# Fixed regions per expert in the dispatched rows, and the meeting of all engines moved ahead of the last group's normalisation

## The reference, cut to what matters

```python
x = x + ga * attn(h)                      # retention and an MLP of 1024: x3 in the kernel
h = _layernorm(x) * (1 + cb) + sb         # h3
probs = softmax(h @ gate_w.T)             # 16 experts
topk_w, topk_idx = top_k(probs, 4)        # weights, then divided by their sum
shared = silu_mul(h @ shared_gate_up.T, 704) @ shared_down.T * sigmoid(h @ shared_gate_vec.T)
sparse = sum over experts e of silu_mul(h @ w_gu[e].T, 176) @ w_d[e].T * combine[:, e]
out = x + gb * (shared + sparse)
```

## Time and profile before

| what | us |
|---|---|
| median of three runs | 632.84 (631.92 to 635.31) |
| the profiled execution, its own time | 636.92 |
| its span (first to last instruction) | 635.1 |
| PE busy, DVE busy, ACT busy, POOL busy | 541.8, 473.5, 283.3, 321.8 |
| mean granted clock of PE | 0.928 of full |

### The profile page before, as it was taken

The page is one execution under the profiler, slowest core; times in us unless marked ns, Lnnn a source line. Parts: engine busy times, 40 slices in busy tenths (PEclk is TensorE's granted clock), DMA queues, the critical chain, the costliest instruction groups (busy, mean ns, idle before and its releaser), DMA issues.

```text
span 635.1 us, 14023 instructions
## 1 busy us (share of the span) xinstructions
PE 541.8 (85%) x4139; PEld 471.7 (74%) x4140; DVE 473.5 (75%) x1197; ACT 283.3 (45%) x696; POOL 321.8 (51%) x390
## 2 busy tenths in 40 slices
PE   4889899999979999994799789977999999999600
PEld 1567677888869889882587568866999999999500
DVE  3588989888743898987675876756777777777478
ACT  3355555556546655441245244425444444444200
POOL 3256776878665474551076757700444444444400
PEclk8889999999999999995789989978999999999855
DMA  9412122224990521112166567686544444442297
GB/s 309 162 57 71 55 73 83 52 74 149 329 311 14 148 76 62 49 58 68 42 186 201 166 212 232 221 252 209 167 133 130 125 132 127 124 131 88 76 382 279
DMA packets 66389, 92.30 MB, mean 145 GB/s; under 512 B 8512, under 2 KB 55360, under 8 KB 66336
## 3 DMA queue, kind: packets, MB, share of 16 engines
q1 hardware_dynamic: 56176, 69.72, 36.2%
q0 software_dynamic: 6864, 18.88, 8.0%
q10 hardware_dynamic: 3296, 3.03, 1.4%
HBM read 53.69 MB, written 35.82 MB: 141 GB/s over the span
## 4 chain that ended last, share of the span: by engine, by line
PE 34%; DVE 8%; issue 4%; DMA 3%; ACT 2%; another core or an unknown queue 1%; SPq 0%; POOL 0%; DVEq 0%; ACTq 0%; POOLq 0%
PE bank L2063 12%; PE bank L1797 5%; PE bank L2081 4%; DVE wda_lo L2028 4%; PE bank L1813 3%; PE bank L2083 3%; PE bank L2047 3%; PE bank L2073 3%; DMA wgu_hi<-results 1%; ACT s_a_hi L1604 1%; DMA stage<-expert_d 1%; DMA stage<-expert_gu 1%; DVE s_a_lo L1720 1%; DMA stage<-shared_d 0%
## 5 line engine op out<-in xcount | busy, mean ns | idle before, releaser
L1931 POOL DMA_INDIRECT results<-yb,xe x79 | 75.8, 959 | 107.1 <-DVE yb L2010 75.6
L1575 POOL DMA_INDIRECT dispatched<-rows,slot x64 | 66.0, 1031 | 40.1 <-issue 17.5
L2063 PE MATMUL bank<-wgu_hi,xT_hi 128*128 x158 | 59.2, 375 | 5.5 <-DVE xT_lo L1991 5.5
L2004 DVE TENSOR_TENSOR e_hT_lo<-bank,e_hT_hi 128x256 fp32r<-128x256 f32 x79 | 33.5, 425 | 32.6 <-issue 20.5
L2063 PE MATMUL bank<-wgu_hi,xT_lo 128*128 x158 | 51.9, 329 | 0.0
L2063 PE MATMUL bank<-wgu_lo,xT_hi 128*128 x158 | 51.9, 329 | 0.0
L736 DVE TENSOR_TENSOR probs<-bank,causal 128x512 f32<-128x512 f32 x64 | 39.8, 684 | 13.6 <-PE bank L926 13.6
L1964 ACT CAST e_hT_hi<-bank 128x256 fp32r<-128x256 f32 x79 | 29.4, 373 | 41.1 <-PE bank L2073 37.9
L1959 ACT ACTIVATE e_sg<-bank 128x176 f32<-128x176 f32 x79 | 25.1, 317 | 50.1 <-PE bank L2063 34.1
L591 POOL TENSOR_TENSOR orms<-omse,neghalf 128x16 f32<-128x16 f32 x16 | 47.1, 2944 | 0.3
L1797 PE MATMUL bank<-h3T_hi,wsg_hi 128*128 128x512 f32 x88 | 38.3, 435 | 6.3 <-DVE hid L1716 2.1
(11 more groups left out here) (234 smaller groups left out, 1854.9 us busy)
## 6 DMA issues: line engine op xcount, KB each, us to landing
dispatched<-fill SPq DMA_DIRECT2D x20, 520.0 KB, 9.0
xe<-dispatched SPq DMA_DIRECT2D x79, 130.0 KB
trig<-t_trig SPq DMA_DIRECT2D x16, 512.0 KB, 3.7
stage<-expert_gu SPq DMA_DIRECT2D x16, 352.0 KB
wgu_hi<-results SPq DMA_DIRECT2D x11, 512.0 KB, 7.7
xt<-L_attn_x SPq DMA_DIRECT2D x32, 128.0 KB, 2.6
wgu_lo<-results SPq DMA_DIRECT2D x5, 512.0 KB, 16.5
x_rows<-h_all SPq DMA_DIRECT2D x16, 128.0 KB, 2.0
```

The lines of the kernel that those rows point to most:

```text
L1575: pool.indirect_dma_start(out=dram["dispatched"], out_offset=bass.IndirectOffsetOnAxis(ap=slot[:, k, t:t + 1], axis=0), in_=rows[:, t, :], ...
L1931: pool.indirect_dma_start(out=dram["results"], out_offset=bass.IndirectOffsetOnAxis(ap=xe[r][:, E:E + 1].bitcast(INT), axis=0), in_=yb[:, ...
L2004: nc.vector.tensor_tensor(hT[1][:, q, :], hT_bank[p][:, 0:2 * P], hT[0][:, q, :].bitcast(F32), ALU.subtract).then_inc(S["h_lo"], 1)
L2063: mm = nc.tensor.matmul(gu_bank[p][:, 0:GU], xT[xn_][:, p, k, :], wgu[wn][:, k, e, :], start=(k == 0 and i == 0), stop=(k == KB - 1 and i ...
```

## The change

Each expert gets a region of its own of REGION = N + P = 2176 rows in `dispatched` (16 regions, and 16 tiles of empty rows behind them). A slot is then the region's start plus the row's rank among the rows of that expert so far, and is known for the first EARLY = 10 tiles as soon as those are ranked. The functions of the row chain move out of `mlp` into `normalised_rows`, which is built twice: for the first block, and again for the second (`last`). The meeting now stands ahead of the row chain of group 3, and that chain is laid between the first blocks of the shared expert. The ranking is in two parts (10 tiles, 6 tiles), as are `slots` and the scatters, which no longer wait for PE's products. The counts are turned into tile numbers by PE with four small products; the 16 steps of `experts_of_tiles` are gone, and each tile has a row number (`tile_row`) that SP reads into a register ahead of each load. Only 4 DMAs write filler at the start. For each expert SP writes 128 rows behind its last one (`fill_up`), at an address from a register, in two DMAs. The splits of the shared down weights go from DVE to POOL. The 24 pieces are 0, 6, 9 and 9 in the four groups.

```diff
+REGION = N + P
+EMPTY = NX * REGION
+EARLY = NT - TPG - 2
-        ("dispatched", (ETILES * P, ROW)), ("results", (N * TOPK + 4 * P, E)), ...
+        ("dispatched", (EMPTY + NX * P, ROW)), ("results", (N * TOPK + (4 + NX) * P, E)), ...
 # mlp, SP
-        for n in range(ETILES // 4):
+        for n in range(NX // 4):
             sp.dma_start(unused[n, :, :, :], fill[:, :, :]).then_inc(s_filled, 16)
-            store(NT - TPG + i, i)
 # mlp, POOL, ACT, DVE and PE: the row chain of group NG - 1 is gone from the end of each
-        for i in range(TPG):
-            inverse_std(NG - 1, i)
...
-        for i in range(TPG):
-            evacuate(NG - 1, i)
...
-        for i in range(TPG):
-            add_residual(NG - 1, i)
-        for i in range(TPG + 1):
-            finish(NG - 1, i)
...
-        for i in range(TPG):
-            transpose_h3(NG - 1, i)
-            route(NG - 1, i)
 # shared_and_dispatch
-        count = [[0, 0, 1, 1, 1, 1], [1] * 6, [1, 2, 1, 2, 1, 1], [1] * 6]
+        count = [[0] * 6, [1] * 6, [2, 1, 2, 1, 2, 1], [2, 1, 2, 1, 2, 1]]
 # SP
+        def fill_up(e):
+            if e == 0:
+                sp.wait_ge(S["free"], 1)
+            row = sp.value_load(first_free[0:1, e:e + 1], min_val=0, max_val=EMPTY)
+            sp.dma_start(dram["dispatched"][bass.ds(row, P), 0:E], gb[:, :]).then_inc(s_filled, 16)
+            with nc.allow_non_contiguous_dma(reason="one index per row"):
+                sp.dma_start(dram["dispatched"][bass.ds(row, P), E:E + 1].bitcast(INT), unfilled[:, e:e + 1]).then_inc(s_filled, 16)
+
         def body(g, q):
             for b in range(NB):
+                if g == 1 and b >= 2:
+                    for e in range((b - 2) * NX // 4, (b - 1) * NX // 4):
+                        fill_up(e)
                 if g and b == 4:
                     for n in range(TPG):
                         store_x4(g - 1, n)
                 for n in pieces(g, b):
                     load_piece(n)
 # POOL
+        last.inverse_std(LG, 0)
+        last.inverse_std(LG, 1)
         pool.wait_ge(S["tab_in"], 64)
+        number(0, near)
+        number(0, far)
+        low_down(0)
+        last.inverse_std(LG, 2)
+        last.inverse_std(LG, 3)
+        low_down(1)
+        send(0, near, 1, 1)
+        low_down(2)
+        send(0, far, 2, 1)
+        for k in range(1, TOPK):
+            number(k, near)
+            send(k, near, 2 * k + 1, k + 1)
...
-                    if n % PACE == 0:
-                        pool.wait_ge(S["g_ps"], n // PACE + 2)
 # DVE
+        def first_blocks():
+            for i in range(TPG):
+                last.add_residual(LG, i)
+            for i in range(2):
+                last.stats(LG, i)
+                last.centre(LG, i)
+            rank_early()
+            last.modulate(LG, 0)
+            last.keep_logits(LG - 1, TPG - 1)
+            last.compare(LG - 1, 1)
+            product(0, 0)
+            slots(0, False)
+            last.stats(LG, 2)
+            last.centre(LG, 2)
+            last.modulate(LG, 1)
+            low_hidden(0, 0)
+            last.choose(LG - 1, 1)
+            last.stats(LG, 3)
+            last.centre(LG, 3)
+            last.modulate(LG, 2)
+            last.modulate(LG, 3)
+            last.low_part(LG, 0)
+            last.keep_logits(LG, 0)
+            product(0, 1)
+            last.low_part(LG, 1)
+            last.keep_logits(LG, 1)
+            low_hidden(0, 1)
+            slots(1, False)
+            last.compare(LG, 0)
+            hidden(0, 2)
+            last.low_part(LG, 2)
+            last.keep_logits(LG, 2)
+            last.choose(LG, 0)
+            slots(2, False)
+            last.low_part(LG, 3)
+            last.keep_logits(LG, 3)
+            last.compare(LG, 1)
+            last.choose(LG, 1)
+
         def route(g, b):
-            if g == 0 and b == 0:
-                bases()
-                slots(0)
-                low_down(0)
...
+            if g == 0 and b == 3:
+                tiles_of_experts()
+                slots(3, False)
+                rank_late()
+                slots(0, True)
             elif g == 0 and b == 4:
+                ends_of_experts()
                 less_best()
+                slots(1, True)
+            elif g == 0:
+                slots(2, True)
             elif g == 1 and b == 0:
+                experts_of_tiles()
                 shared_gate()
+                slots(3, True)
             elif g == 1 and b < 5:
-                experts_of_tiles(b - 1)
                 weigh(b - 1)
 # PE: group 0
+        first_product(0, 0)
+        early_ranks()
+        pe.wait_ge(S["first"], 1)
+        last.transpose_h3(LG, 0)
+        first_product(0, 1)
+        last.transpose_h3(LG, 1)
+        last.route(LG, 0)
+        second_product(0, 0, 0)
+        first_product(0, 2)
+        last.transpose_h3(LG, 2)
+        last.route(LG, 1)
+        second_product(0, 1, 0)
+        last.transpose_h3(LG, 3)
+        last.route(LG, 2)
+        first_product(0, 3)
+        last.route(LG, 3)
+        second_product(0, 2, 0)
+        first_product(0, 4)
+        count()
+        first_product(0, 5)
+        second_product(0, 3, 0)
+        base_of_experts()
 # experts_and_combine, SP
-                sp.dma_start(xe[r][:, :], dispatched[j, :, :]).then_inc(s_in[r], 16)
+                row = sp.value_load(tile_row[0:1, bass.ds(j, 1)], min_val=0, max_val=EMPTY + (NX - 1) * P)
+                sp.dma_start(xe[r][:, 0:E + 1], dispatched[bass.ds(row, P), 0:E + 1]).then_inc(s_in[r], 16)
```

More of the change, by code:

```diff
@@ L1078, in mlp @@
     ahead = Ahead()
+    R = normalised_rows(nc, sem, wait, alone, neghalf, ident, modb, h_all, near, early, h3T, rows, logits, order, chosen, before_tile,
+                        ebefore, x3_tiles, outs, b_tr, b_lg, 0, S)
     def chunk(n):
@@ L1435, in shared_and_dispatch, with rows_from @@
-def shared_and_dispatch(nc, io, sb, sem, wait, alone, bank, gb, weights, tile_expert, h3T, rows, logits,
-                        order, chosen, before_tile, ebefore, wsg, wgu, dram, s_filled, s_down, home):
+        R.route(NG - 2, TPG - 1)
+    def rows_from(first):
+        return normalised_rows(nc, sem, wait, alone, neghalf, ident, modb, h_all, near, early, h3T, rows, logits, order, chosen, before_tile,
+                               ebefore, x3_tiles, outs, b_tr, b_lg, first, None)
+    return Stage(sync, gpsimd, scalar, vector, tensor, S, ahead, rows_from)
@@ L1438, in shared_and_dispatch @@
+def shared_and_dispatch(nc, io, sb, sem, wait, alone, bank, gb, weights, tile_expert, tile_row, h3T, rows, logits,
+                        order, chosen, before_tile, ebefore, wsg, wgu, dram, s_filled, s_down, home, last):
     INT = mybir.dt.int32
     NB, LAST = SBLOCKS, SBLOCKS - 1
+    bank = [bank[n] for n in (0, 3, 5, 7, 1, 4, 2, 6)]
+    LG = NG - 1
     RING, SKEW = 3, 2
@@ L1765, in body @@
                 hidden(g, b)
-                if isinstance(g, int):
-                    route(g, b)
+                route(g, b)
+                if g == 1 and b == 0:
+                    for i in range(TPG):
+                        dve.wait_ge(last.S[f"row_out{i}"], 16)
                 for n in pieces(g, b):
@@ L1829, in tensor, with experts_and_combine @@
             second_product(NG - 1, b, (NG - 1) % 2)
-    done = dict(S, store_last=store_last, wda=wda, pieces=DOWN + NX // 2)
+    done = dict(S, store_last=store_last, wda=wda, pieces=NX + NX // 2)
     return Stage(sync, gpsimd, scalar, vector, tensor, done)
-def experts_and_combine(nc, io, sem, wait, alone, bank, ident, gb, weights, tile_expert, wgu, rows, dram, s_down, out, home, before):
+def experts_and_combine(nc, io, sem, wait, alone, bank, ident, gb, weights, tile_expert, tile_row, wgu, rows, dram, s_down, out, home, before):
     INT = mybir.dt.int32
+    bank = [bank[n] for n in (0, 3, 5, 7, 1, 4, 2, 6)]
     XR, YR = 16, 4
```

548 lines of the change are left out of this document (312 added, 236 removed).

## The result

The changed kernel takes 639.36 us (median of 6 runs, 637.62 to 640.46) where the kernel before takes 633.05 (6 runs beside them, 631.88 to 635.31): a ratio of 1.0091, with a 95% interval of 1.0066 to 1.0115. The forecast was 620.8 with a range of 614.5 to 629.

A forecast was written before the change was run, and what follows sets the result against it. DVE was taken to bound group 0 and, before the change, group 1; PE group 2 and the experts' loop. -16.5 + 4.7 - 4.7 + 3.0 + 1.0 + 0.5 = -12.0 us, so 632.8 becomes 620.8, range 614.5 to 629.

The forecast's parts named there:

- The start of the second block: With the row chain of group 3 behind the meeting, the shared expert starts at 286.8 for 303.3: minus 16.5 us.
- Group 0: First group of the shared expert, now carrying the row chain: DVE binds, 45.0 us where it took 40.3, plus 4.7.
- The clock: Rival: PE often falls to its lower clock in group 0, 3 to 7 us more; chance 0.18 for 624 to 629.
- Group 1: Second group of the shared expert: without `experts_of_tiles` DVE has less work, 26.2 us for 30.9, minus 4.7.
- SP's fill-ups: Twelve between loads of pieces 5 to 8 stall ACT, then PE, by 12 F - 12.6; F = 1.3 gives plus 3.0.
- Groups 2 and 3: Nine pieces each for eight and six: nothing in group 2, plus 1.0 us (0 to 3) in group 3.
- Start of the experts: Four register reads on SP precede the remaining down weights' load, mostly covered by scatters ending earlier: plus 0.5 us.
- The rival on the other side: Fill-ups choke the pieces' loads: at F = 2.3 the stall is 15 us and the gain gone; chance 0.10.

The follow-up runs named there:

- e7: The kernel of e1 with the three splits of the shared down weights moved back from POOL to DVE: 627.92 us, ratio 0.9933 to the kernel before.
- e4: The kernel before, unchanged, profiled a second time: 631.83 us for the profiled execution, span 630.0 us.
- e1: The changed kernel without fill-ups in the second block, filler written ahead over fixed rows (not general): 627.87 us, ratio 0.9934 to the kernel before.
- e6: The kernel of e1 with the piece loads of groups 2 and 3 cut to 32 of 704 columns, ACT's and DVE's work kept: 618.61 us (one run).
- e9: The kernel of e8 with the pieces as 3, 6, 8, 7 over the four groups instead of 0, 8, 8, 8: 625.20 us, ratio 0.988 to the kernel before.
- e5: The kernel of e1 with the pieces as 8, 8, 8 in groups 1 to 3 instead of 6, 9, 9: 628.05 us, ratio 0.9916 to the kernel before.
- e8: The changed kernel with fill-ups on ACT's queue, one behind each silu from block (1,0), and pieces as in e5: 628.43 us, ratio 0.9928 to the kernel before.

## Why the prediction was wrong

- **The start of the second block**, -16.5: right, 285.7 for 286.8.
- **Group 0**, 45.0 us: nearly right, 45.8, but by errors that cancel: DVE was busy 36.2 where I counted 32.4 and 1.0 for the port, and waited 9.6 where I counted 11.6. The port conflicts cost 3.0 for my 1.0 (e7), and DVE's waits for the router, for which I took 2.4, came to one of 0.95 us. PE's work I had put at some 28 us, and it was busy 39.6: the stretch holds eight first products and not six, and the earlier trace rows has 38.16 for the same stretch of before. That DVE sets the pace came true (PE waits for DVE's results by 1.10, 2.22 and 1.88 us at 290.71, 296.12 and 305.20), but with less room than I thought. The comparison was worse than the term: the profiled execution of before had a group 0 of 40.3, and e4 has 38.5. I took the excess of that execution off the final sum alone, and not off the stage where part of it lay.
- **The clock** as rival: fell. PE's granted clock over group 0 was 0.96. It was at 0.50 from about 298 to 301 us, after idle times of 1.1 and 2.2 us, and at 1.00 nearly everywhere else. With 39.6 us of work in place of 28 PE had fewer gaps than this rival assumed.
- **Group 1**, -4.7: right when the fill-ups are away (e1, 26.4 for 26.2).
- **SP's fill-ups**, +3.0: this is the first step that failed, and only in the size of F, the time that one fill-up takes on SP's queue. The formula 12 F - 12.6 gives 9.0 with the F of 1.8 that the starts in groups of four show (342.37 to 347.75, three steps), and e1 measures 8.5 in group 1 and 11.5 on the median. The sum of the durations was right, though not each of them: the register read 0.33, its arithmetic and assertion 0.17 (for my 0.05), and two DMAs of 0.33 (for my 0.47) with 0.07 of register work each add up to the 1.3 that I took. What I left out is the time between instructions on the queue, another 0.5 for nine of them. I had F = 1.9 as the upper end and took the lower third, because I priced the sequence as a sum of its durations. The Trainium skill (DMA: Bandwidth & Descriptors, Latency and other measured facts) gives a floor of some 600 ns for the read; the 16 reads here have a median of 0.33 (0.28 to 0.69), so its F of 1.6 is nearer to 1.8 than mine, but not for its reason.
- **Groups 2 and 3**, +1.0: the second step that failed, and the larger one. They cost 2.9 and 4.5 more than in the first profile of before, 3.4 and 5.3 more than in e4. I argued from busy time: DVE has 8 us free, ACT 14. True, and e6 shows that the work does fit. But a piece is a loop of 5.4 to 6.0 us (load 3.6 to 4.3, ACT 0.78, DVE 0.89, and the time until each comes to it in its order), with two halves of the stage, and a block with two pieces has some 4.4 us in group 2 and 3.7 in group 3. Behind a wait of 2.94 us in group 3 PE's clock fell as well (0.91 over the group); over group 2, whose longest wait was 2.69, it stayed at 1.00. I wrote that "their loads share two buffers", and put 0 to 3 on it without working out that loop. That the four pieces leave group 0 I booked as 3.6 us won for DVE; e9 shows the other side of it, 7.5 us later for three pieces against 1.75 saved.
- **Start of the experts**, +0.5: +1.3 to +2.0 from the end of the shared expert to the last `yb`, against the two profiles of before. Four tile loads with their reads take 4.04 us on SP ahead of the down weights, issued at 421.77. But ACT waited only 0.32 us for these weights, so their late issue explains little of it. No run isolates it.
- **The rival on the other side** named the right place and the wrong threshold: the gain being gone from F = 2.3 on holds only while groups 2 and 3 cost 1.0. With the 7.4 us that they cost against the first profile, the sum is +0.4 at F = 1.8: -16.5 + 4.7 - 4.7 + 9.0 + 7.4 + 0.5. The medians say +6.3.
- **The whole, against e4.** My -12.0 and the +5.8 of the spans lie 17.8 us apart: 7.7 in groups 2 and 3 (+8.7 for +1.0), 5.7 in group 1 with its fill-ups (+4.0 for -1.7), 2.6 in group 0 (+7.3 for +4.7), and 1.8 from the experts on (+2.3 for +0.5). Even with F and the loop right (+0.4) I would have been 5 to 6 us too low: the profile that I worked from is 5.1 us longer than e4's, 1.8 of it in group 0, and I set my new group 0 against that one.

What is open: e9, which is general, takes 625.2 us and has groups of 47.7 and 27.0 us left where e4 has 38.5 and 25.7. A third buffer for the stage, which would test the loop directly, was not run; that two buffers are what makes the landing bind rests on the chain, on e5 and on e9. Nor was the traffic of the scatters ever taken away.

## What to carry to other kernels

When work moves between stages, follow each load's loop from the release of its buffer to the next release, and set it against the time that the stage gives to as many loads as there are buffers, block by block: here one turn of both buffers takes 5.4 to 6.0 us, and the blocks with two pieces have 4.4 in group 2 and 3.7 in group 3. An average over the stage hides it, and free time on the engines says nothing about it. Price a sequence on a DMA queue by the distance between starts, gaps included, and keep it off the queue that feeds the stage: here the 16 fill-ups cost 11.5 us on SP between the loads (e1 against the changed kernel) and nothing that can be measured on ACT's queue (e8 against e5). And take the base for a sum from a profile whose time is the median, stage by stage.

## What the hardware showed that was not expected

- The nine small instructions of a fill-up (a register read, arithmetic, an assertion, two DMAs) have 1.3 us of durations and take 1.66 to 2.04 us on SP's queue, for the twelve between the loads.
- To halve a load's landing took far more than half of its bytes away: 352 KB landed in 3.3 to 4.3 us (medians of the stretches looked at), 16 KB in 1.8 to 2.0. The Trainium skill (DMA: Bandwidth & Descriptors, Anatomy of one DMA) gives about 2 us that no size takes away, for DMAs issued from GpSimd. The 1.8 and 2.0 us of these 16 KB loads from SP are near it.
- Each of three DVE steps of two or more inputs that met a POOL `tensor_tensor` took 0.94 to 1.11 us longer, whatever its own length (0.43 to 0.69): about twice the 0.5 that I had read from the earlier trace rows, and 63 to 86% of POOL's 1.27 to 1.56 us.
- A wait of PE can cost more than its length: behind the 4.36 us at 357.02 PE ran at the lower level (granted clock 0.50) until about 362, and the twelve products of a block took 5.49 us, for 3.02 at 285.74 with the clock at 1.00. Over group 2, where PE was idle for 5.3 us in pieces of up to 2.69, the clock was 1.00.
